# Gram matmuls placed inside the looks of a recommendation kernel

## The reference

```python
e = stack([tbl_k[ids[:, k]] for k in range(26)], axis=1)          # 2048 x 26 x 128
combined = concatenate([dense[:, None, :], e], axis=1)            # 2048 x 27 x 128
inter = einsum('bnd,bmd->bnm', combined, combined)[:, triu_i, triu_j]
h = concatenate([dense, inter, dense], axis=1)                    # 2048 x 607
h = maximum(h @ W_top1 + b_top1, 0)                               # 512
h = maximum(h @ W_top2 + b_top2, 0)                               # 256
y = h @ W_top3                                                    # 1
```

## Time and profile before

| | |
|---|---|
| median of 3 runs | 381.85 us (380.86 to 382.14) |
| the profiled execution's own time | 384.91 us |
| its span | 382.8 us, 13108 instructions |
| mean granted TensorE clock | 0.991 |
| PE busy | 341.9 us, 6048 matmul records |
| weight loads (PEld) busy | 304.2 us |
| DVE, ACT, POOL busy | 193.2, 125.5, 252.1 us |

### The profile page before, as it was taken

One profiled execution on the slowest core, in us unless ns is written; L12 is line 12 of the kernel. 1 busy time (PEld: TensorE's weight loads), 2 busy tenths in 40 slices (PEclk: granted clock), 3 DMA queues, 4 the chain that ended last, 5 costly groups with the idle time before them and its releaser, 6 DMA issues.

```text
span 382.8 us, 13108 instructions
## 1 busy us (share of the span) xinstructions
PE 341.9 (89%) x6048; PEld 304.2 (79%) x6048; DVE 193.2 (50%) x94; ACT 125.5 (33%) x211; POOL 252.1 (66%) x267
## 2 busy tenths in 40 slices
PE   0788878984999999999999999999999999999995
PEld 0687767883898898898988898889988898977763
DVE  2899996565424396228833495238742595100000
ACT  2235433332132341334322342323322333343122
POOL 3777887777777777777777777777777777500200
PEclk9999999999799999999999999999999999999999
DMA  8975698254322537225632536234622533420400
GB/s 205 222 210 166 170 301 250 58 195 126 126 80 58 193 82 200 58 80 177 149 119 58 194 92 190 58 120 140 187 79 58 193 89 86 144 73 27 154 13 0
DMA packets 30868, 49.57 MB, mean 129 GB/s; under 512 B 17499, under 2 KB 17635, under 8 KB 30686
## 3 DMA queue, kind: packets, MB, share of 16 engines
q1 hardware_dynamic: 22350, 31.68, 27.0%
q0 software_dynamic: 8320, 16.92, 16.8%
q10 hardware_dynamic: 144, 0.13, 0.1%
HBM read 38.21 MB, written 10.49 MB: 127 GB/s over the span
## 4 chain that ended last, share of the span: by engine, by line
PE 72%; POOL 14%; issue 6%; DMA 4%; DVE 2%; ACT 1%; DVEq 0%
PE look_ps L309 28%; POOL rows L290 14%; PE mid_ps L339 13%; PE layer_ps L356 11%; PE layer_ps L365 7%; PE mid_ps L321 7%; PE layer_ps L353 4%; DMA rows<-in_table,index 3%; DVE match L463 2%; PE layer_ps L372 2%; DMA index<-in_index 1%; ACT hidden L528 0%; ACT hidden L534 0%; ACT turned L501 0%; ACT turned L512 0%
## 5 line engine op out<-in xcount | busy, mean ns | idle before, releaser
L290 POOL DMA_INDIRECT rows<-in_table,index x256 | 248.8, 972 | 82.3 <-issue 75.0
L463 DVE TENSOR_TENSOR match<-look_ids,row_number_ps 125x2048 fp32r<-125x2048 int32 x80 | 181.7, 2286 | 132.2 <-PE look_ps L309 122.3
L309 PE MATMUL look_ps<-match,table_high 125*128 125x256 f32 x640 | 165.7, 296 | 20.2 <-DVE table_low L471 18.1
L309 PE MATMUL look_ps<-match,table_low 125*128 125x256 f32 x640 | 159.4, 286 | 0.1
L309 PEld LDWEIGHTS look_ps<-match,table_high 125*128 125x128 f32 x640 | 124.8, 195 | 25.0 <-issue 16.0
L309 PEld LDWEIGHTS look_ps<-match,table_low 125*128 125x128 f32 x640 | 125.1, 195 | 0.0
L339 PEld LDWEIGHTS mid_ps<-turned 128*32 128x32 f32 x4096 | 45.3, 109 | 19.1 <-issue 15.3
L339 PE MATMUL mid_ps<-turned 128*32 128x27 f32 x4096 | 54.4, 195 | 5.5 <-issue 1.7
L501 ACT COPY turned<-look_ps 128x512 f32<-128x512 f32 x40 | 31.9, 798 | 73.5 <-PE look_ps L309 72.2
L508 ACT COPY turned<-mid_ps 128x512 f32<-128x512 f32 x64 | 42.8, 672 | 19.7 <-PE mid_ps L321 19.5
L321 PE MATMUL mid_ps<-identity,rows 128*128 128x128 f32 x256 | 40.6, 283 | 9.4 <-DMA rows<-in_table,index 8.5
(11 more groups left out here) (21 smaller groups left out, 44.8 us busy)
## 6 DMA issues: line engine op xcount, KB each, us to landing
look_ids<-in_look_rows SPq DMA_DIRECT2D x40, 256.0 KB, 4.4
scratch<-grams SPq DMA_DIRECT2D x8, 864.0 KB, 4.4
rows<-in_table,index POOLq DMA_INDIRECT x256
scratch<-grams SPq DMA_DIRECT2D x8, 416.0 KB, 5.2
pairs<-scratch SPq DMA_DIRECT2D x92, 29.2 KB
grams<-in_table SPq DMA_DIRECT2D x4, 448.0 KB
pairs<-in_table SPq DMA_DIRECT2D x3, 448.0 KB
hidden<-in_table SPq DMA_DIRECT2D x3, 448.0 KB
```

The source lines that it names most:

```text
L290: pool.indirect_dma_start(out=rows[j % 2][:, at, :], out_offset=None, in_=tables[GATHERED[at]], in_offset=bass.IndirectOffsetOnAxis(ap=ind ...
L309: last = nc.tensor.matmul(look_ps[pair % 2][:, r % 2, :], part[0:table_rows, r, c, :], match[number % 2][0:table_rows, c, :], start=(c == ...
L463: nc.vector.tensor_tensor(match[number % 2][0:table_rows], look_ids[b][0:table_rows, r % 2].unsqueeze(1).broadcast_to(shape), row_number_p ...
```

## The change

Each gram step of groups 0 to 6 moves into a look: behind each of the 16 look matmuls come four samples (4 matmuls, 8 records) of the step. The look's own completion is signalled by its last matmul as before; the gram's waits stand ahead of the look's first matmul. The order of a step becomes turn, look with gram, piece of a layer, and ScalarE takes the turn ahead of the gram. The gram steps of group 7 stay in one piece. In the last group's end, output 3 of layer 1 and layer 2 of group 5 move ahead of the last four turns, and layer 3 ahead of gram step 3. The common order of turns and grams is now made by a generator, `mid_order`.

```diff
@@ -161,23 +161,26 @@
             return 2 * number + 2


-
-
-        PERIOD = TURNS + STEPS
+        def mid_order():
+            yield from (("turn", 0, k) for k in range(TURNS))
+            for g in range(1, groups):
+                for k in range(STEPS):
+                    yield "turn", g, k
+                    yield "gram", g - 1, k
+                if g + 1 < groups:
+                    yield from (("turn", g, k) for k in range(STEPS, TURNS))
+
+            yield from (("gram", g, 0), ("gram", g, 1))
+            yield from (("turn", g, k) for k in range(STEPS, TURNS))
+            yield from (("gram", g, 2), ("gram", g, 3))
+
+        mid_place = {step: number for number, step in enumerate(mid_order())}
...
@@ -297,20 +300,26 @@

         @block.tensor
         def _(pe):
-            def look(g, r):
+            def look(g, r, step=None, every=1):
+
                 number, pair = look_number(g, r), pair_number(g, r // 2)
                 if g == 0:
                     pe.wait_ge(tables_split, r + 1)

                 after(pe, looked, pair - 1)
                 pe.wait_ge(match_ready, number + 1)
+                if step is not None:
+                    gram_ready(g - 1, step)
                 for c in range(PARTS):
-                    for part in (table_high, table_low):
+                    for h, part in enumerate((table_high, table_low)):
                         last = nc.tensor.matmul(look_ps[pair % 2][:, r % 2, :], part[0:table_rows, r, c, :],
                                                 match[number % 2][0:table_rows, c, :],
                                                 start=(c == 0 and part is table_high),
                                                 stop=(c == PARTS - 1 and part is table_low))
-                last.then_inc(look_done, 1)
+                        if c == PARTS - 1 and part is table_low:
+                            last.then_inc(look_done, 1)
+                        if step is not None and (2 * c + h + 1) % every == 0:
+                            four_samples(g - 1, step, (2 * c + h) // every)

             def turn(g, k):
                 j, u = g * TILES + k // UNITS, k % UNITS
@@ -322,8 +331,7 @@
                                                rows[j % 2][:, u * UNIT_OF + n, :], identity[:])
                 last.then_inc(turn_done, 1)

-            def gram(g, k):
-                number = gram_number(g, k)
+            def gram_ready(g, k):
                 if k == 0:

                     pe.wait_ge(mid_out, turn_number(g, TURNS - 1 if g + 1 < groups else UNITS - 1) + 1)
@@ -331,15 +339,23 @@
                     pe.wait_ge(dense_put, g + 1)
                 if k == STEPS // TILES and g + 1 == groups:
                     pe.wait_ge(mid_out, turn_number(g, TURNS - 1) + 1)
-                after(pe, mid_out, number - 2)
+                after(pe, mid_out, gram_number(g, k) - 2)
+
+            def four_samples(g, k, i):
+
+                x = k * IN_STEP + i
+                for s in range(QUADS):
+                    n = (x // BLOCK * P + s * BLOCK + x % BLOCK) * FEATURES
+                    last = nc.tensor.matmul(
+                        mid_ps[gram_number(g, k) % 3][s * ROW:(s + 1) * ROW, i * FEATURES:(i + 1) * FEATURES],
+                        turned[g % 2][:, n:n + ROW], turned[g % 2][:, n:n + FEATURES], start=True, stop=True)
+                if i == IN_STEP - 1:
+                    last.then_inc(gram_done, 1)
+
+            def gram(g, k):
+                gram_ready(g, k)
                 for i in range(IN_STEP):
-                    for s in range(QUADS):
-                        x = k * IN_STEP + i
-                        n = (x // BLOCK * P + s * BLOCK + x % BLOCK) * FEATURES
-                        last = nc.tensor.matmul(
-                            mid_ps[number % 3][s * ROW:(s + 1) * ROW, i * FEATURES:(i + 1) * FEATURES],
-                            turned[g % 2][:, n:n + ROW], turned[g % 2][:, n:n + FEATURES], start=True, stop=True)
-                last.then_inc(gram_done, 1)
+                    four_samples(g, k, i)
...
@@ -392,26 +408,22 @@
                 if g == 2:
                     pe.wait_ge(weights_summed, 1)
                     pe.wait_ge(weights_in, WEIGHT_DMAS)
-                gram(g - 1, 0)
                 turn(g, 0)
-                look(g, 6)
+                look(g, 6, step=0)
                 if g >= 2:
                     layer1(g - 2, 0)
                     layer1(g - 2, 1)
-                gram(g - 1, 1)
                 turn(g, 1)
-                look(g, 7)
+                look(g, 7, step=1)
                 if g >= 2:
...
@@ -427,23 +439,20 @@

             g = groups - 1
             for k in range(STEPS):
-                gram(g - 1, k)
                 turn(g, k)
-                look(g, AHEAD + k)
+                look(g, AHEAD + k, step=k)
             layer1(g - 2, 0)
             layer1(g - 2, 1)
             gram(g, 0)
             layer1(g - 2, 2)
+            layer1(g - 2, 3)
             gram(g, 1)
-            turn(g, 4)
-            turn(g, 5)
-            turn(g, 6)
-            turn(g, 7)
-            layer1(g - 2, 3)
+            layer2(g - 2)
+            for k in range(STEPS, TURNS):
+                turn(g, k)
             gram(g, 2)
-            layer2(g - 2)
+            layer3(g - 2)
             gram(g, 3)
-            layer3(g - 2)
...
@@ -563,21 +572,21 @@
             act.wait_ge(weights_summed, 1)
             act.wait_ge(weights_in, WEIGHT_DMAS)
             for g in range(1, groups - 1):
+                take_turned(g, 0)
                 take_gram(g - 1, 0)
-                take_turned(g, 0)
                 if g >= 2:
                     relu1(g - 2, 0)
+                take_turned(g, 1)
                 take_gram(g - 1, 1)
-                take_turned(g, 1)
                 take_look(g, 3)
                 if g >= 2:
                     relu1(g - 2, 1)
+                take_turned(g, 2)
                 take_gram(g - 1, 2)
...
             take_turned(g, 2)
             put_dense(g)
+            take_gram(g - 1, 2)
+            take_turned(g, 3)
             take_gram(g - 1, 3)
-            take_turned(g, 3)
             take_look(g, 4)
             relu1(g - 2, 0)
             take_gram(g, 0)
+            relu1(g - 2, 1)
             take_gram(g, 1)
-            take_turned(g, 4)
-            take_turned(g, 5)
-            take_turned(g, 6)
-            take_turned(g, 7)
-            relu1(g - 2, 1)
+            relu2(g - 2)
+            for k in range(STEPS, TURNS):
+                take_turned(g, k)
             take_gram(g, 2)
-            relu2(g - 2)
+            copy_y(g - 2)
             take_gram(g, 3)
-            copy_y(g - 2)
```

More of the change, by code:

```diff
@@ L161, in pair_end @@
             return 2 * number + 2
-        PERIOD = TURNS + STEPS
-        def turn_number(g, k):
[L169 to L174, removed]
+        def mid_order():
[10 more added lines that the diff above has]
+        mid_place = {step: number for number, step in enumerate(mid_order())}
+        def turn_number(g, k):
+            return mid_place["turn", g, k]
         def gram_number(g, k):
[L177 to L180, removed]
+            return mid_place["gram", g, k]
         block = ctx.enter_context(nc.Block())
@@ L406, in _ @@
                     layer1(g - 2, 3)
-                gram(g - 1, 2)
                 turn(g, 2)
-                look(g, 8)
+                look(g, 8, step=2)
                 if g >= 2:
                     layer2(g - 2)
-                gram(g - 1, 3)
                 turn(g, 3)
-                look(g, 9)
+                look(g, 9, step=3)
                 if g >= 2:
@@ L574, in _ @@
                     relu1(g - 2, 1)
+                take_turned(g, 2)
                 take_gram(g - 1, 2)
-                take_turned(g, 2)
                 if g >= 2:
                     relu2(g - 2)
+                take_turned(g, 3)
                 take_gram(g - 1, 3)
-                take_turned(g, 3)
                 take_look(g, 4)
@@ L592, in _ @@
             g = groups - 1
+            take_turned(g, 0)
             take_gram(g - 1, 0)
-            take_turned(g, 0)
+            take_turned(g, 1)
             take_gram(g - 1, 1)
-            take_turned(g, 1)
             take_look(g, 3)
-            take_gram(g - 1, 2)
             take_turned(g, 2)
             put_dense(g)
+            take_gram(g - 1, 2)
+            take_turned(g, 3)
             take_gram(g - 1, 3)
-            take_turned(g, 3)
             take_look(g, 4)
```

## The result

The changed kernel takes 602.9 us (599.97 to 603.46, 4 runs) against 381.93 for the one before, a ratio of 1.578 (95% interval 1.573 to 1.583): 221 us slower. The forecast was slower, but at 487 us, and the range ended at 540.

What follows compares the result with a forecast made beforehand. PE was taken to bound the kernel. Groups 2 to 6 add 83 us, group 7 15.8, group 1 6 and the tail 0.7: 105.5 on the median 381.85, so 487 us, range 440 to 540.

Steps and rivals of the forecast that it cites:

- The seam: On PE, between 128-column look and 32-column gram matmuls: 0.09 more, no early gram load, 0.12 back, 0.10 exposed wide load.
- Slot: One look matmul with 8 gram records behind it, in interleaved steps: 0.50 us, against 0.22 before.
- Rivals A: In each slot the exposed wide load hides or the drain is partly shared: slot 0.40, 445 us; chance 0.13.
- C: Rival: the seam belongs to the queue's boundary, gram slips between look matmuls: slot under about 0.24, 366 us; chance 0.09.
- The clock: PE's granted clock in the interleaved steps: the forecast's sum gave a fall no cost, leaving it to rival B.
- Forecast 0.65 at 487: Whole kernel: the predicted time of 487 us (450 to 520), given a chance of 0.65.
- rival B: PE's clock falls to 1.2 GHz in all steps, each slot gaining 0.1 to 0.5: 532 to 710, middle 590 us; chance 0.12.
- the mild edge of B: The low end of rival B's 532 to 710 us, which the range of 440 to 540 takes in.
- Group 1: Its four interleaved steps, partly covered by slack from its gathers: the next period's first gram at 108.9, not 102.9: +6.
- Turns in front: Transposes ahead of the gram in each step: banks, copies and gathers keep up, costing nothing.
- Tail: End of the last group: two seam pairs less, -0.3, gram 2 waiting for ScalarE's copies, +1.0: together +0.7 us.
- The long slots hide this wholly: Gram's idle stops for its own instructions vanish in interleaved steps; already in the sum, undisturbed step 1.10 against some 1.6 us.

Runs made afterwards that it cites:

- e4: Changed kernel with one matmul of 128 columns (2 records) behind each interleaved look matmul in place of the four of 32 columns: 447.07 us, one run.
- e6: Changed kernel with each look matmul of the interleaved looks issued twice, 448 matmuls more: 549.56 us, one run.
- e8: Against e1, only gram step 0 of each of groups 1 to 6 interleaved, the other steps in one piece: 431.16 us, one run.
- e1: Changed kernel without the interleaving: gram in one piece between turn and look, new order and tail kept: 387.74 us, ratio 1.014.
- e9: Kernel before the change with the new tail alone: 385.34 us, ratio 1.006.
- e11: Kernel before, with layer 3 beside the gram, each gram step in two halves around the turn, and ScalarE copying the turn first: 378.07 us, ratio 0.989.
- e3: Changed kernel with 32 samples behind each eighth look matmul in place of four behind each: 386.84 us, ratio 1.013.
- e7: Changed kernel with each look matmul of the interleaved looks issued three times: 639.0 us, one run.

## Why the prediction was wrong

- **The seam: right.** Slot 0.50 predicted, 0.51 measured; 0.31 from look to gram and 0.20 back; the load does not run ahead. e4 shows that the width is the cause. A full-clock period was to be 59; e6 gives 67.1 - 64 x 0.12 = 59.4. TensorEngine Tiling (Array Packing) of the Trainium skill, Key Properties, says that a change of the tiling mode drains TensorE; the traces agree, at some 0.2 us a pair and 0.10 of exposed load. Rivals A (0.40) and C (under 0.24) are out.
- **The clock: the step that failed.** "Forecast 0.65 at 487" rests on seams alone, and rival B got 0.12 since nothing so thin was in the trace. The step that failed is the clock's term, put at nothing in all 28 steps; by e6 it is some 107 of the 221 us (602.9 against 496), while the seams' own sum, 487, comes within 9 us of that 496. B was the case: its middle, 590 us, is 2% from the result, but in part by luck. B had every slot at half clock and nothing beside the slots. Measured, a slot is 0.26 longer at half clock, between the 0.1 and the 0.5 given; 192 of 420 pay it, some 50 us, and the rest of the 107 lies in the layers, looks and turns behind them, as in e8. The range took in only "the mild edge of B", because I took a missing row as evidence against, where it is evidence for neither.
- **Group 1: +6 predicted.** From about 103 before, the start of the next period went to 130.1: +27. e6, which ran group 1 at full clock, gives 119.8 - 64 x 0.12 = 112, +9 for the seams; the other 18 are the clock, at half from 63.7 to 118.3.
- **Turns in front: costed at nothing, cost some 3 us, 0.6 a period** (e1 less e9; 43.0 against 42.4). Behind the gram stands a look, whose exposed load is 0.10, and no longer a turn, whose is 0.06 (0.66 behind a gram in the earlier trace rows and e11, 0.60 behind a look in e1). That is 0.2 of the 0.6. The rest would be longer stops for instructions: e1's grams of the middle periods take 1.70 on the mean, those before 1.59. This wasn't tested, and single traces of the same order differ by as much (e9's middle periods have 42.8).
- **Tail: +0.7 predicted, about +2 measured** (e9). From layer 2's last matmul to gram 2 it took 3.5 us where 4.0 were predicted. Missed was the stop of 1.17 us when two gram steps stand nearly side by side, 0.6 more for the two together; the rest is not accounted for.
- **"The long slots hide this wholly"**, of the stops: true, and worth 0.5 us a step, but e11's halves give 0.4 of it, for one pair of seams more instead of fifteen.

## What to carry to other kernels

Before interleaving small matmuls into big ones on TensorE, read from the trace what one change between 128 and 32 columns costs there and back, and multiply: here 0.2 us and an exposed load of 0.1 each. Then ask how much of the new slot PE still streams; if the trace has no stretch as thin, the half clock is an open case and belongs in the range. If the aim is to shorten stops for instructions, two pieces around the transposes gained 1% here (e11), and two pieces inside the look nothing (e3).

## What the runs showed that I had not expected

- In the middle periods the granted clock falls to half though PE is shown busy for 72.89 of 73.20 us, and doing more can be faster: 549.6 us with 448 matmuls added, against 602.9.
- The dense work behind a thin step runs at half clock too: e8's clock came back some 5 us after the step.
- The same interleaved slots ran at half for 82 us when the clock had fallen ahead of them, and at full clock in every later period (e7). What brings it back is left open.
- 128 gram records in a row mostly stop for instructions (30 of 32 steps before, 0.5 us on the mean). Of e11's 64 in a row, 41 of 56 ran through in at most 0.6 us, some 9 ns a record; of e3's, 24 of 56. So the length of the row is not the whole of it.
